# A fourth item buffer for VectorE in a windowed-attention and mixture-of-experts kernel

## The chip, the cores and the metric

The kernel runs on one core of one Trainium2 chip. Its metric is the device time in microseconds of one execution, from the first to the last instruction with what lies around them.

## The reference

The input is x of 8 x 1024 tokens with 128 channels. After a layer norm, the result is x plus an attention plus a mixture of experts. The attention is unusual: there are no queries and keys, but for each of 16 heads and each token a window of 64 earlier tokens, and for each pair a small network.

```
disp_win = windows(xn @ W_disp)            # 64 offsets per token, 16 values per head
strain   = disp_win - disp                 # token by token, offset by offset
bond     = gelu(strain @ W_strain + rel_emb @ W_pos) @ W_bond
damage   = sigmoid(gelu(strain @ W_dmg + b_dmg) @ W_dmg_out + b_dmg_out)
weights  = softmax(bond - 10 * damage)     # over the 64 offsets, masked at the start
attn     = (weights * val_win).sum(offsets) @ W_cproj
ffn      = sum over the 8 best of 160 experts of gate * silu(xn @ Wg) @ Wd, + a shared expert
out      = x + attn + ffn
```

## The kernel before

There is one program per engine, ordered by hand and tied by counting semaphores. It has a **token phase** (layer norm, projections, routing, to some 310 us), a short slot computation, the **first half** of the attention (half 0, 349 to some 1600 us), the **expert phase**, and the **second half** (half 1, from 2160 us). The token phase also writes zeros over xslot_dram, which the scatters of half 0 later fill.

An attention half handles 8 chunks of 512 tokens, each in two **steps**, one for each group of 8 heads. Steps are counted through, 0 to 15 in half 0 and 16 to 31 in half 1. The first and last steps of a half are written out; the middle ten are a loop of two steps (an even and an odd one) run five times, so that in each half four even steps, 6, 8, 10, 12 and 22, 24, 26, 28, begin behind a taken branch.

A step has 16 **items**, n = 0 to 15. An item is 8 offsets of one of the two networks (even n: bond, odd n: damage), a tile of 128 x 4096 fp32, 16 KB in each partition. It goes through three engines:

- the **subtraction** writes the item into a buffer: n%4 = 3 on GpSimd (u_pool, L954), the other three of four on VectorE (u_dve): as eight instructions of 512 columns, which also add the positional term (L1098, "STT" below), or as one of 4096 (L1093, "TT"); in half 1 items 6 and 14 use the latter and get the term in ScalarE (BIASED);
- ScalarE applies the gelu in place (L1021, L1023, or L1017 for those two);
- TensorE multiplies by the small output vectors (L1190, 8 matmuls, shown as x16) and raises item_done. It takes items in order, so item_done counts items 0, 1, 2, ... of all steps.

A VectorE buffer is free again when TensorE has done the item in it. The rule before is one buffer for each place in the group of four, and a wait for the item four places back:

```
return u_dve[:, (n % 4 - sum(q < n % 4 for q in on_pool))]      # item_buffer
return n - 3                                                    # buffer_free
```

Between items the engines do the rest of the attention, at fixed places of the same order. The places that matter here:

- **here** (L1168), on TensorE behind item 12: it puts the tokens' own values of the next step into ps_here, from which VectorE subtracts. It waits for all of this step's VectorE subtractions, and item 0 of the next step waits for it (here_done).
- **lg** (L1111), on VectorE behind items 0, 4, 8, 12: joins bond and damage logits of a group of four items; waits for ScalarE's tanh (L1005).
- **turn 0** (L1230, L1236), on TensorE behind item 4: brings logits of the step before into token order, into the one PSUM tile ps_u; turns 1 to 3 (L1238) stand behind items 5, 6, 7, and each waits until VectorE has emptied ps_u (tokens_in).
- **mx** and **ml** (L1120, L1125), on VectorE at places 7, 8, 9, 10: maximum and subtraction of the softmax, each behind its turn. The subtractions of items 8, 9 and 10 stand between them. Ahead of the first, at place 6, stand two small instructions (oinv L1129, o_sb L1133), and in half 1 the sum of eight gathered expert rows (add_routed, L1064, L1068, L1074), which stands behind item 14 too.
- **band transposes** (L1253), on TensorE from place 8: they use ps_u too, and the first waits for the fourth ml. ScalarE copies them out (L1037) behind its gelu of item 9 and on.

The zero-fill of xslot_dram (L315) is issued by SyncE once in each of the 16 chunks of the token phase and counted by slots_zeroed, for which GpSimd waits at the start of half 0.

Of the kernel before, what the change touches and what calls it, by code (L numbers as in the profile page):

```python
# [19 lines left out]
F32 = mybir.dt.float32  # L20
# [7 lines left out]
P = 128  # L28
# [11 lines left out]
def moe_attention_layer(nc, x, w_dispT, w_val, relT, w_strain, w_pos, w_bond, w_dmg, b_dmg,  # L40
# [28 lines left out]
    with ExitStack() as ctx:  # L69
# [42 lines left out]
        def sb(name, shape, dt=F32, c=ctx):  # L112
            return c.enter_context(nc.sbuf_tensor(name, shape, dt))
# [1 line left out]
        ident = sb("ident", [P, P])  # L115
        gates_all = sb("gates_all", [P, NBLK * TOPK])
        slots_all = sb("slots_all", [P, NBLK * TOPK])
        w1 = sb("w1", [P, 2 * HG, P])
        wval_sb = sb("wval_sb", [P, C])
        wr_sb = sb("wr_sb", [P, NE])  # L120
        bias_sb = sb("bias_sb", [P, NE])
        wgs_sb = sb("wgs_sb", [P, I])
        wds_sb = sb("wds_sb", [I, C])
        wc_sb = sb("wc_sb", [P, C])
# [8 lines left out]
        tile_id = sb("tile_id", [P, 6])  # L133
        mhalf = sb("mhalf", [P, J])

        zero = sb("zero", [P, 2048])
        slots_zeroed = sem("slots_zeroed")
        routing = ctx.enter_context(ExitStack())
        ranks_all = sb("ranks_all", [P, NCH * J, NE], F32, routing)
# [109 lines left out]
        with ExitStack() as c:  # L249
# [48 lines left out]
            with nc.Block() as block:  # L298
                @block.sync
                def _(sp):  # L300
                    def load(it, u):
                        sp.dma_start(xin[:, u], chunk_rows(x_rows, it)).then_inc(x_loaded[u], 16)

                    def body(k, last=False):
                        for u in range(2):
                            it = k * 2 + u
                            if not (last and u == 1):

                                if some(k + u):
                                    sp.wait_ge(x_free[1 - u], k + u)  # L310
                                load(it + 1, 1 - u)
                            sp.wait_ge(xn_ready, J * it + J)
                            sp.dma_start(chunk_rows(xn_dram, it), xn[:]).then_inc(stored["xn"], 16)

                            sp.dma_start(xslot_dram[bass.ds(it * ZR * P, ZR * P), :]  # L315
                                         .rearrange("(p n r) c -> p n (r c)", p=P, n=3),
                                         zero[:, 0:ZR * C // 3].unsqueeze(1).to_broadcast([P, 3, ZR * C // 3]))\
                                .then_inc(slots_zeroed, 16)
                            sp.wait_ge(part_ready, it + 1)
                            sp.dma_start(chunk_rows(part_dram, it), part_sb[:]).then_inc(stored["part"], 16)  # L320

                    load(0, 0)
                    ahead(sp, NCH // 2, body)
                    for s in stored.values():
                        sp.wait_ge(s, 16 * NCH)

                @block.gpsimd
                def _(pool):
# [307 lines left out]
        routing.close()  # L636


        NI = 16
        CH = 4  # L640
        NSTEP = 2 * NCH
# [24 lines left out]
        gate_done, hidden_done, down_done = sem("gate_done"), sem("hidden_done"), sem("down_done")  # L666
        ys_ready = sem("ys_ready")

        u_dve = sb("u_dve", [P, 3, 8, TC])
        u_pool = sb("u_pool", [P, 2, 8, TC])  # L670
        s_win = sb("s_win", [P, HG, 2, SW])
        tanh_sb = sb("tanh_sb", [P, 2, TC])
# [27 lines left out]
        def attention(half):  # L700
# [40 lines left out]
            def item_buffer(n):  # L741

                if n % 4 in on_pool:
                    return u_pool[:, (pool_of[n] - 1) % 2]
                return u_dve[:, (n % 4 - sum(q < n % 4 for q in on_pool))]

            def buffer_free(n):

                if n % 4 in on_pool:
                    return n + 1 - 8 // NP  # L750
                return n - 3

            def sync(sp):
                def load_windows(b, tc, it, par):
# [154 lines left out]
            def gpsimd(pool):  # L909
                if half == 0:  # L910
                    pool.memset(v_one[:], 1.0).then_inc(v_zeroed, 1)
                    pool.wait_ge(v_zeroed, 1)
                    pool.wait_ge(slots_zeroed, 16 * NCH)

                def spread(it):

                    pool.wait_ge(v_loaded, 16 * 2 * J * (it + 1))

                    if some(16 * it):
                        pool.wait_ge(av_done, 16 * it)  # L920
                        pool.sem_inc(held, 1)
                    pool.tensor_copy(v_one[:, :, :, 0:HS], v_raw[:].rearrange("p w (h e) -> p w h e", h=H))\
                        .then_inc(v_spread, 1)

                def route(s, par, j):

                    pool.wait_ge(slots_here, s + 1)
                    pool.sem_inc(held, 1)
                    if half == 0:
                        pool.wait_ge(rows_in, 16 * (s + 1))  # L930
                        pool.sem_inc(held, 1)
                        for i in range(j * TOPK, (j + 1) * TOPK):
                            pool.indirect_dma_start(  # L933
                                xslot_dram, bass.IndirectOffsetOnAxis(ap=slot_now[:, par, i:i + 1], axis=0),
                                xr[:, par, j, :], None).then_inc(scattered[par], 16)
                    else:

                        if some(s - first):
                            pool.wait_ge(sum_round, 2 * ROUND * (s - first - 1) + ROUND * (j // 2 + 1))
                            pool.sem_inc(held, 1)  # L940
                        for i in range(j * TOPK, (j + 1) * TOPK):
                            pool.indirect_dma_start(  # L942
                                yg[:, i, :], None, yslot_dram,
                                bass.IndirectOffsetOnAxis(ap=slot_now[:, par, i:i + 1], axis=0)).then_inc(gathered[j], 16)

                def step(s, it, par, st):
                    for n in range(NI):
                        cgrp, d0, ty = offsets(n)
                        if "i" in st and n % 4 in on_pool:
                            if pool_of[n] == 1:  # L950
                                pool.wait_ge(win_loaded[par], 32 * it + 32)
                            if some(NI * s + buffer_free(n)):
                                pool.wait_ge(item_done, NI * s + buffer_free(n))
                            pool.tensor_tensor(  # L954
                                item_buffer(n), windows(par, ty, d0, 8),
                                s_win[:, par, ty, PAD:PAD + TC].unsqueeze(1).to_broadcast([P, 8, TC]),
                                ALU.subtract).then_inc(sub_pool, 1)
                        if "y" in st and n == 12:

                            if some(it - 1):  # L960
                                pool.wait_ge(y_copied, it - 1)
                            if some(16 * (it - 1)):
                                pool.wait_ge(part_loaded, 16 * (it - 1))
                            pool.tensor_tensor(y_sb[:], y_sb[:], part_t[:], ALU.add).then_inc(y_ready, 1)
                        if "i" in st and n % 4 == 3:
                            route(s, par, n // 4)
                        if "a" in st and n == 7 and par == 0:
                            spread(it - 1)

                steps(pool, step)  # L970
# [522 lines left out]
```

## Time and profile before

| | us |
|---|---|
| median of 3 runs | 3539.15 |
| lowest, highest | 3538.04, 3539.51 |
| the profiled execution, its own time | 3547.54 |
| its span, first to last instruction | 3545.7 |
| VectorE busy | 2789.8 (79%) |
| ScalarE busy | 2505.1 (71%) |
| TensorE busy | 2462.7 (69%) |
| GpSimd busy | 2329.5 (66%) |

Times in the trace are counted from the start of the span. A matmul's end is modelled. The profiler names what ended an engine's idle time behind an arrow; "issue" stands where it knows nothing that the engine waited for.

### The profile page before, as it was taken

To read this page: it belongs to the slowest core of one execution; us is meant where nothing else is said; L and a number is where in the kernel's file an instruction comes from. 1 tells how busy PE (TensorE), PEld (TensorE's weight loads), DVE (VectorE), ACT (ScalarE), POOL (GpSimd) and SP (SyncE) were. 2 spreads that over 40 slices of the span, in tenths; PEclk is the share of its full clock that TensorE was granted. 3 is DMA by queue.
4 is the path that set the end of the run, shared out by engine and by line. 5 is a ranking of instruction groups with operands and counts; after the bars stand their busy time and mean duration, and the time that the engine had idled before them with its cause. 6 is when DMAs were issued, how large, how long until landed. Compare 5 with 4: busy or idle time off the path is not lost.

```text
span 3545.7 us, 64286 instructions
## 1 busy us (share of the span) xinstructions
PE 2462.7 (69%) x21226; PEld 1194.3 (34%) x21226; DVE 2789.8 (79%) x4286; ACT 2505.1 (71%) x1717; POOL 2329.5 (66%) x1603
## 2 busy tenths in 40 slices
PE   4663567766677767677888886676777676767666
PEld 2441112222222222225667663222222222222224
DVE  6888998888898888873333447999989999999981
ACT  1110898988888888883333335989898988888982
POOL 1221888887888787863434346888787777777760
PEclk9896888888888889879999998888887888888985
DMA  6774122222222222227888883223232222223222
GB/s 246 286 291 149 41 72 83 81 91 82 99 84 81 77 85 85 87 75 223 243 245 243 243 245 107 84 82 94 81 108 77 87 75 85 80 85 90 81 83 75
DMA packets 366243, 435.33 MB, mean 123 GB/s; under 512 B 48673, under 2 KB 282993, under 8 KB 366066
## 3 DMA queue, kind: packets, MB, share of 16 engines
q1 hardware_dynamic: 284658, 278.53, 25.2%
q0 software_dynamic: 57216, 143.22, 12.3%
q10 hardware_dynamic: 24192, 11.02, 1.1%
q8 instruction: 136, 2.23, 0.3%
q14 instruction: 41, 0.34, 0.0%
HBM read 233.83 MB, written 198.77 MB: 122 GB/s over the span
## 4 chain that ended last, share of the span: by engine, by line
ACT 22%; DVE 20%; PE 16%; issue 15%; SPq 10%; DMA 2%; ACTq 0%; DVEq 0%; POOL 0%; POOLq 0%
PE ps L1190 11%; DVE u_dve L1098 8%; DVE u_dve L1093 7%; ACT u_dve L1023 7%; SPq L1297 5%; ACT u_pool L1021 5%; ACT u_dve L1021 4%; SPq L1298 3%; PE ps L1253 3%; SPq L1309 2%; ACT at_sb L1037 2%; DVE mx L1120 2%; DVE ps L1068 1%; ACT L1029 1%; DVE ml L1125 1%
## 5 line engine op out<-in xcount | busy, mean ns | idle before, releaser
L1098 DVE SCALAR_TENSOR_TENSOR u_dve<-s_win,rpos,ps_here 128x512 f32<-128x512 f32 x1792 | 1198.1, 742 | 161.3 <-PE ps L1190 112.4
L1190 PE MATMUL ps<-u_dve,wsel 128*32 128x512 f32 x6144 | 953.5, 749 | 404.4 <-ACT u_dve L1021 207.8
L954 POOL TENSOR_TENSOR u_pool<-s_win 128x4096 f32<-128x4096 f32 x128 | 1021.9, 7984 | 167.7 <-PE ps L1190 162.2
L1023 ACT ACTIVATE u_dve<-u_dve 128x4096 f32<-128x4096 f32 x224 | 810.1, 3616 | 57.4 <-DVE u_dve L1098 57.1
L1093 DVE TENSOR_TENSOR u_dve<-s_win,ps_here 128x4096 f32<-128x4096 f32 x160 | 703.8, 4416 | 62.9 <-PE ps L1190 62.9
L933 POOL DMA_INDIRECT xslot_dram<-xr,slot_now x512 | 497.4, 972 | 146.9 <-issue 145.4
L942 POOL DMA_INDIRECT yg<-yslot_dram,slot_now x512 | 485.7, 949 | 157.9 <-issue 147.0
L1021 ACT ACTIVATE u_dve<-u_dve,bdmg_sb 128x4096 f32<-128x4096 f32 x128 | 474.9, 3710 | 12.2 <-DVE u_dve L1093 11.7
L1021 ACT ACTIVATE u_pool<-u_pool,bdmg_sb 128x4096 f32<-128x4096 f32 x128 | 474.1, 3704 | 0.0
L1190 PEld LDWEIGHTS ps<-u_dve,wsel 128*32 128x32 f32 x6144 | 190.6, 125 | 816.0 <-issue 524.0
L1388 DVE TENSOR_TENSOR u_pool<-u_pool,ps 128x512 f32<-128x512 f32 x168 | 115.6, 688 | 338.3 <-ACT u_pool L1373 338.3
L1190 PE MATMUL ps<-u_pool,wsel 128*32 128x512 f32 x2048 | 279.2, 668 | 100.0 <-ACT u_pool L1021 100.0
L1037 ACT ACTIVATE at_sb<-ps 128x512 f32<-128x512 f32 x256 | 150.9, 590 | 240.6 <-PE ps L1253 177.0
L1366 ACT ACTIVATE u_pool<-ps_here 128x512 f32<-128x512 f32 x168 | 100.3, 597 | 280.7 <-PE ps_here L1320 280.7
L1253 PE MATMUL ps<-ident,band 128*128 128x128 f32 x1024 | 210.0, 337 | 123.4 <-issue 102.2
L1253 PEld LDWEIGHTS ps<-ident,band 128*128 128x128 f32 x1024 | 148.8, 199 | 387.6 <-issue 349.5
L1403 POOL DMA_DIRECT2D yslot_dram<-u_dve x168 | 128.5, 765 | 215.0 <-DVE u_dve L1394 185.3
L1238 PE MATMUL ps<-ident,lg 128*128 128x128 f32 x384 | 75.9, 330 | 182.0 <-DVE ml L1125 182.0
L1298 POOL DMA_DIRECT2D u_dve<-in_w_expert x168 | 90.4, 538 | 151.5 <-issue 105.8
L1158 PEld LDWEIGHTS ps<-v_one,at_sb 128*64 128x64 f32 x4096 | 156.3, 151 | 97.6 <-issue 77.3
L1346 PE MATMUL ps<-u_dve,u_pool 64*128 64x64 f32 x2688 | 187.1, 279 | 0.4 <-DVE u_pool L1388 0.4
L1333 PE MATMUL ps<-u_pool,u_dve 128*64 128x128 f32 x2688 | 186.5, 282 | 0.0
(144 smaller groups left out, 2929.2 us busy)
## 6 DMA issues: line engine op xcount, KB each, us to landing
band<-band_dram SPq DMA_DIRECT2D x32, 2048.0 KB
xslot_dram<-zero SPq DMA_DIRECT2D x16, 2688.0 KB, 9.1
u_dve<-xslot_dram SPq DMA_DIRECT2D x168, 256.0 KB, 3.5
yslot_dram<-u_dve POOLq DMA_DIRECT2D x168, 256.0 KB, 3.3
band_dram<-ml SPq DMA_DIRECT2D x64, 512.0 KB
u_dve<-in_w_expert SPq DMA_DIRECT2D x336, 64.0 KB, 2.8
s_win<-s_dram SPq DMA_DIRECT2D x64, 288.0 KB
s_dram<-s_sb POOLq DMA_DIRECT2D x16, 1024.0 KB, 4.7
```

What stands on the lines that cost most here:

```text
L933: pool.indirect_dma_start(xslot_dram, bass.IndirectOffsetOnAxis(ap=slot_now[:, par, i:i + 1], axis=0), xr[:, par, j, :], None).then_inc(sc ...
L942: pool.indirect_dma_start(yg[:, i, :], None, yslot_dram, bass.IndirectOffsetOnAxis(ap=slot_now[:, par, i:i + 1], axis=0)).then_inc(gathere ...
L954: pool.tensor_tensor(item_buffer(n), windows(par, ty, d0, 8), s_win[:, par, ty, PAD:PAD + TC].unsqueeze(1).to_broadcast([P, 8, TC]), ALU.s ...
L1021: act.activation(u, u, ACT.Gelu, bias=bdmg_sb[:]).then_inc(gelu_done, 1)
L1023: act.activation(u, u, ACT.Gelu).then_inc(gelu_done, 1)
L1037: act.activation(at_sb[:, k % 2].rearrange("p i t -> p (i t)"), ps_u[:], ACT.Copy)\
L1093: last = dve.tensor_tensor(item_buffer(n), windows(par, ty, d0, 8), here.unsqueeze(1).to_broadcast([P, 8, TC]), ALU.subtract)
L1098: last = dve.scalar_tensor_tensor(out=item_buffer(n)[:, d, :], in0=s_win[:, par, ty, d0 + d + 1:d0 + d + 1 + TC], scalar=rpos[:, d0 + d:d0 ...
L1190: last = pe.matmul(logit[32 * g:32 * g + 32, :], wsel[:, ty, q, :], item_buffer(n)[:, d, :], start=(q == 0), stop=(q == 3))
L1253: last = pe.transpose(ps_u[:, i * P:(i + 1) * P], band[:, k // 2, 4 * (k % 2) + i:BANDW:HH], ident[:])
L1298: e.dma_start(we[:, u, i, :], w_expert[bass.ds(row, 1)].rearrange("e p f -> p (e f)"))\
L1346: last = pe.matmul(ps_z[:, u % 2, half, i * I:(i + 1) * I], hs[rows, u % 2, i * P:(i + 1) * P], we[rows, u, i, I:2 * I], start=True, stop= ...
```

## The change

VectorE gets a fourth buffer. Its twelve items of a step take the four buffers in turn (items 0, 1, 2, 4 use buffers 0 to 3, items 5, 6, 8, 9 again, then 10, 12, 13, 14), and each waits for the item that was in its buffer, the fourth before it among VectorE's own. In terms of n: items 0, 4, 8, 12 waited for the item four places back and now wait for the one six back; the others waited four back and now wait for the one five back.

The room comes from four weight tiles and the zero tile of the token phase, which are allocated in a scope of their own that is closed before the attention's tiles are placed. For that the zero-fill must be over by then, so SyncE waits for slots_zeroed at the end of the token phase, and GpSimd no longer does at the start of half 0.

```
@@ allocations
-        w1 = sb("w1", [P, 2 * HG, P])
-        wval_sb = sb("wval_sb", [P, C])
-        wr_sb = sb("wr_sb", [P, NE])
-        bias_sb = sb("bias_sb", [P, NE])
...
-        zero = sb("zero", [P, 2048])
+        start = ctx.enter_context(ExitStack())
+        w1 = sb("w1", [P, 2 * HG, P], F32, start)
+        wval_sb = sb("wval_sb", [P, C], F32, start)
+        wr_sb = sb("wr_sb", [P, NE], F32, start)
+        bias_sb = sb("bias_sb", [P, NE], F32, start)
+        zero = sb("zero", [P, 2048], F32, start)
@@ end of the token phase, SyncE
                     for s in stored.values():
                         sp.wait_ge(s, 16 * NCH)
+                    sp.wait_ge(slots_zeroed, 16 * NCH)
@@ before the attention
         routing.close()
+        start.close()
...
-        u_dve = sb("u_dve", [P, 3, 8, TC])
+        u_dve = sb("u_dve", [P, 4, 8, TC])
@@ item_buffer
-                return u_dve[:, (n % 4 - sum(q < n % 4 for q in on_pool))]
+                return u_dve[:, (dve_of[n] - 1) % 4]
@@ buffer_free
-                return n - 3
+                return max(m for m in range(-NI, n) if m % 4 not in on_pool
+                           and (m // NI * ND + dve_of[m % NI]) == dve_of[n] - 4) + 1
@@ start of half 0, GpSimd
                     pool.wait_ge(v_zeroed, 1)
-                    pool.wait_ge(slots_zeroed, 16 * NCH)
```

No engine's instructions change their order. What moves is the waits. VectorE at the start of step 0, items 0 to 5, before (item 4 is the first row that waits for item_done):

```order
L1098 SCALAR_TENSOR_TENSOR u_dve<-s_win,rpos,ps_here 128x512 [waits here_done,win_loaded0]
L1098 SCALAR_TENSOR_TENSOR u_dve<-s_win,rpos,ps_here 128x512 x7
L1093 TENSOR_TENSOR u_dve<-s_win,ps_here 128x4096
L1098 SCALAR_TENSOR_TENSOR u_dve<-s_win,rpos,ps_here 128x512 x8
L1098 SCALAR_TENSOR_TENSOR u_dve<-s_win,rpos,ps_here 128x512 [waits item_done]
L1098 SCALAR_TENSOR_TENSOR u_dve<-s_win,rpos,ps_here 128x512 x7
L1093 TENSOR_TENSOR u_dve<-s_win,ps_here 128x4096 [waits item_done]
```

and now (the lines are three further down in the file):

```order
L1101 SCALAR_TENSOR_TENSOR u_dve<-s_win,rpos,ps_here 128x512 [waits here_done,win_loaded0]
L1101 SCALAR_TENSOR_TENSOR u_dve<-s_win,rpos,ps_here 128x512 x7
L1096 TENSOR_TENSOR u_dve<-s_win,ps_here 128x4096
L1101 SCALAR_TENSOR_TENSOR u_dve<-s_win,rpos,ps_here 128x512 x16
L1096 TENSOR_TENSOR u_dve<-s_win,ps_here 128x4096 [waits item_done]
```

Items 2 and 4 now stand in one row of sixteen without a wait, and item 5 is the first that waits. In all later steps every item still waits for item_done, for an earlier count, and item 0 still waits for here_done.

## Rows read from the trace of the kernel before

**Rows 1.** Page, part 1: busy time of each engine, share of the span.
```profile
PE 2462.7 (69%) x21226; PEld 1194.3 (34%) x21226; DVE 2789.8 (79%) x4286; ACT 2505.1 (71%) x1717; POOL 2329.5 (66%) x1603
```

**Rows 2.** Waits of VectorE over the span: us in total, times, longest us.
```profile
DVE u_dve L1098 <- PE ps L1190: 112.4, 43, 8.1
DVE u_dve L1093 <- PE ps L1190: 62.9, 40, 3.1
```

**Rows 3.** Timeline, VectorE, step 10: start us, us, instruction, [idle before, releaser].
```profile
1107.60 5.36 DVE L1098 SCALAR_TENSOR_TENSOR u_dve<-s_win,rpos,ps_here 128x512 f32<-128x512 f32 x8 [2.25 <-PE ps_here L1168]
1112.87 0.68 DVE L1111 SCALAR_TENSOR_TENSOR lg<-tanh_sb,ps 128x512 f32<-128x512 f32 x1
...
1133.22 5.36 DVE L1098 SCALAR_TENSOR_TENSOR u_dve<-s_win,rpos,ps_here 128x512 f32<-128x512 f32 x8 [6.29 <-PE ps L1190]
...
1139.09 4.42 DVE L1093 TENSOR_TENSOR u_dve<-s_win,ps_here 128x4096 f32<-128x4096 f32 x1
1143.42 5.35 DVE L1098 SCALAR_TENSOR_TENSOR u_dve<-s_win,rpos,ps_here 128x512 f32<-128x512 f32 x8
...
1149.42 0.68 DVE L1120 TENSOR_REDUCE mx<-ps 128x8 f32<-128x512 f32 x1
```

**Rows 4.** Timeline, TensorE, step 10: items 14, 0, 1, turn 0, first band transpose.
```profile
1117.98 3.51 PE L1190 MATMUL ps<-u_dve,wsel 128*32 128x512 f32 x16
...
1129.51 3.64 PE L1190 MATMUL ps<-u_dve,wsel 128*32 128x512 f32 x16 [3.75 <-issue]
...
1135.18 3.44 PE L1190 MATMUL ps<-u_dve,wsel 128*32 128x512 f32 x16 [1.06 <-ACT u_dve L1023]
...
1145.37 1.05 PE L1236 MATMUL ps<-ident,lg 128*128 128x128 f32 x8
...
1170.43 0.88 PE L1253 MATMUL ps<-ident,band 128*128 128x128 f32 x3 [4.13 <-issue]
```

**Rows 5.** Timeline, ScalarE, step 10: gelu of item 4.
```profile
1138.61 3.62 ACT L1023 ACTIVATE u_dve<-u_dve 128x4096 f32<-128x4096 f32 x1
```

**Rows 6.** Timeline, VectorE, step 24: item 0, start of add_routed, first mx.
```profile
2800.50 5.35 DVE L1098 SCALAR_TENSOR_TENSOR u_dve<-s_win,rpos,ps_here 128x512 f32<-128x512 f32 x8 [0.28 <-issue]
...
2838.99 0.60 DVE L1064 TENSOR_SCALAR ps<-yg,gate_now 128x128 f32<-128x128 f32 x2
...
2843.58 0.68 DVE L1120 TENSOR_REDUCE mx<-ps 128x8 f32<-128x512 f32 x1
```

**Rows 7.** Timeline, TensorE, step 24: items 14, 0, 1, turn 0.
```profile
2809.89 1.92 PE L1190 MATMUL ps<-u_dve,wsel 128*32 128x512 f32 x16 [0.83 <-ACT u_dve L1017]
...
2820.52 3.16 PE L1190 MATMUL ps<-u_dve,wsel 128*32 128x512 f32 x16 [3.41 <-issue]
...
2824.56 1.93 PE L1190 MATMUL ps<-u_dve,wsel 128*32 128x512 f32 x16
...
2836.04 1.05 PE L1236 MATMUL ps<-ident,lg 128*128 128x128 f32 x8
```

**Rows 8.** Timeline, turn 0 and first mx of steps 17 and 31.
```profile
2269.70 1.05 PE L1236 MATMUL ps<-ident,lg 128*128 128x128 f32 x8
2273.03 0.68 DVE L1120 TENSOR_REDUCE mx<-ps 128x8 f32<-128x512 f32 x1
...
3409.79 1.05 PE L1236 MATMUL ps<-ident,lg 128*128 128x128 f32 x8
3412.01 0.68 DVE L1120 TENSOR_REDUCE mx<-ps 128x8 f32<-128x512 f32 x1
```

**Rows 9.** Busy time by stretch, steps 22 and 24: length, PE, PEld, DVE, ACT, POOL, granted clock.
```profile
2630.00:2716.00 86.00, 59.96 (x447) 22.07 (x444) 75.97 (x106) 72.32 (x48) 63.92 (x38) 0.78 0.28 81
2797.00:2879.00 82.00, 54.63 (x446) 20.53 (x442) 73.82 (x98) 70.78 (x48) 62.84 (x38) 0.88 0.29 85
```

**Rows 10.** Timeline, SyncE's queue: last zero-fill and the last store of the token phase.
```profile
291.19 0.57 SPq L315 DMA_DIRECT2D xslot_dram<-zero  x1
306.71 0.38 SPq L320 DMA_DIRECT2D part_dram<-part_sb  x1
```

## The prediction, written before the changed kernel ran

> **What bounds the kernel now.** I read the page's busy times first, then VectorE's waits, then the timeline of single steps. VectorE is busiest, but with 79% of the span it has holes [rows 1]. Of these the change can touch only the waits for an item's buffer: 112.4 us ahead of the STT subtractions and 62.9 us ahead of the TT ones, 175.3 us together [rows 2]. That is a ceiling and not a gain, since VectorE waits again for other things; the question is where its lateness holds someone up.
>
> So follow one step. Step 10 begins with item 0 at 1107.60, when ps_here is there. VectorE then waits 6.29 us for the buffer of item 4 [rows 3]. That wait ends with item 0 on TensorE, at 1129.51 + 3.64 = 1133.15 [rows 4]. TensorE was late with it because of 3.75 us put down to "issue" [rows 4]; steps 6, 8, 10, 12 and 22, 24, 26, 28, all behind the loop's branch, have it, and the same place in the straight-line even steps has not. VectorE is then busy without a hole until its first mx at 1149.42 [rows 3]. But turn 0, for which that mx waits, was done at 1145.37 + 1.05 = 1146.42 [rows 4]. VectorE is **3.00 us late** at the one place where it is the bound. From here four mx and ml pairs with items 8, 9, 10 between them run on VectorE without a hole, while TensorE waits for each; the first band transpose starts at 1170.43 after 4.13 us of idleness [rows 4], 21.0 us behind the first mx. Behind it ScalarE leads again, up to the next turn 0: it does the gelu of item 4 at 1138.61, at the end of item 3's, and the turn follows item 4 [rows 5]. So a step's period is ScalarE's chain up to turn 0, plus what VectorE is late, plus the fixed 21 us and the way to the next "here". In every step the distances other than the lateness differ by at most 2 to 4 us.
>
> I took turn 0's end and the start of the first mx in all 31 steps that have them. A step without lateness has 0.04 us between them. **Lateness:** steps 6, 8, 10, 12: 3.27, 2.87, 3.00, 3.01. Steps 17, 18, 19, 20, 21, 30, 31: 2.28, 3.10, 1.32, 3.09, 1.31, 2.69, 1.17 (the first is 2273.03 less 2270.75, the last 3412.01 less 3410.84) [rows 8]. Step 22: 6.92; 24, 26, 28: 6.49, 6.52, 6.56 (2843.58 less 2837.09 in step 24 [rows 6, 7]). Steps 23, 25, 27, 29: 0.29 or 0.30. All others 0.04, but for steps 1 and 2 with 0.6, where VectorE works without a buffer wait.
>
> **The change part by part.** *The fourth buffer, step 10.* An STT item takes 5.27 us from start to start, lg 0.68, a TT item 4.33 (1139.09 to 1143.42) [rows 3]. Item 0 at 1107.60, with its lg to 1113.6. Item 1 asks for item 12, done before "here": to 1117.9. Item 2 asks for item 13, which stands ahead of item 14 (from 1117.98 [rows 4]): to 1123.2. Item 4 asks for item 14, done at 1121.49 [rows 4], no wait: with lg to 1129.1, against 1139.1 before. Item 5 asks for item 0, done at 1133.15: to 1137.5. Item 6 asks for item 1, done at 1135.18 + 3.44 = 1138.62 [rows 4]: to 1143.9. The two small instructions (0.73, from 1143.42 + 5.27 to 1149.42) end at 1144.7. Turn 0 is done at 1146.42, so the first mx starts there: **all 3.0 us of lateness go**, and 1.7 us of waiting at turn 0 take their place. Steps 6, 8, 12 come out alike: 12.15 less 4 x 0.04 = 12.0 us.
>
> *Step 24.* Item 0 at 2800.50 [rows 6], lg to 2806.4, item 1 to 2810.8, item 2 to 2816.0, item 4 (item 14 done at 2811.81 [rows 7]) with lg to 2822.0, item 5 from the end of item 0 at 2823.68 to 2828.0, item 6 (TT here; item 1 done at 2826.49) to 2832.3, the small ones to 2833.1, add_routed 4.59 (2838.99 to 2843.58 [rows 6]) to 2837.7. Turn 0 is done at 2837.09, so 0.6 of 6.49 stays and 5.9 go. Steps 24, 26, 28: 17.6. Step 22 by the same steps: 5.6.
>
> *The seven steps with 1.17 to 3.10.* The same working clears turn 0 by 1 us or more in each: 14.96 less 7 x 0.04 = 14.7. The four with 0.29: 1.0. **Sum: 12.0 + 17.6 + 5.6 + 14.7 + 1.0 = 50.9 us.**
>
> *Why no more.* Item 0 of a step still waits for "here", behind item 12, so VectorE's lead ends with each step. Steps with no lateness gain nothing: their buffer waits become waits at turn 0. Behind the first mx the places are fixed.
>
> *What hides the rest.* The earlier writes lie beside ScalarE and GpSimd, as they do now. Per step GpSimd is busy 62.8 to 63.9 us of 82 to 86 [rows 9]; a step of 77 still holds that and its issue gaps. SyncE's new wait costs nothing: the last zero-fill is issued at 291.19, and a store that SyncE waits for anyway only at 306.71 [rows 10]; if a fill took longer than those 15 us, the rest would show once. GpSimd's dropped wait was long fulfilled. No instruction is added or moved, and the expert phase still uses buffers 0 to 2.
>
> *A rule beside the 3.75 us.* In the steps behind the branch item 0 is late by 3.75 and 3.41 us of "issue" [rows 4, 7], and I leave that in. The Trainium skill ("Runtime: NRT & Kernel Launch", Instruction fetch mechanics) says that a taken branch to a target outside the window held makes the engine fetch the page before it goes on. By that rule the stall is TensorE's own and stays, which gives the sum above; were it a hidden wait for VectorE, the sum would be that of the second rival.
>
> **From the sum to the time.** The sum is made in an execution of 3547.54 us by its own time (span 3545.7), 8.4 over the median; the steps have no reason to differ, so I subtract from the median: 3539.15 - 50.9 = **3488 us**.
>
> **The rivals.** *Forecast*, 42 to 62 us saved. The one unknown is TensorE's clock. Step 22 ran at a granted clock of 0.78, step 24 at 0.88 (1 being 2.4 GHz, one half 1.2) [rows 9]; counted from "here", with which these stretches begin, turn 0 ends at 41.9 us in one and 40.0 in the other, and VectorE would be ready for it at 43.2 or 40.7. If 24, 26, 28 fell to 22's level, 3 x 2.5 us of the gain would go; if eight or nine steps rose to 24's, 1.9 us each, 16 us would come on top. Chance 0.67.
>
> *More:* the stall behind the branch goes too. At most 8 x 3.6 = 29 us more, 3459. Against it: it stands only behind the branch. With the lucky clocks (3472) chance 0.08.
>
> *Part:* ScalarE or TensorE slips as VectorE comes early (an item at 3.64 us instead of 1.92 ahead of turn 0 costs 1.7 [rows 4, 7]), and half the gain stays, 3514. For it: items 0 and 1 in step 10 did run at 1.2 GHz behind an idle stretch. Chance 0.17.
>
> *Nothing:* VectorE's new lead is held elsewhere, at "here" or in a numbering of the buffers that gives no slack. But the order shows a wait less at items 2 and 4, and 12 items fit four buffers three times, so the counts match across steps. 3532 to 3546, chance 0.05.
>
> *Slower:* TensorE is given 1.2 GHz in item 4 and turn 0 of most steps. Item 4 would take 1.7 us more, the turn's two parts (twice about 1.0 [rows 4]) up to 2.0 more: 3.7 us a step, 115 us in 31 steps, 3603. From the 14th such step on it outweighs the gain. What speaks against it: between turn 0 and the band transposes TensorE will idle less and not more. The Trainium skill ("TensorE: Matmul & The Clock Gate", Part 1) ties the clock to how busy the array has been lately, so by it the clock would sooner rise, which no row here can settle. Chance 0.03.
>
> **The numbers.** A measurement tells 0.2%, 7 us, from no change. Faster: 0.67 + 0.08 + 0.17 = 0.92; same 0.05; slower 0.03. The range goes from the lucky clocks, 3472, to just over half the gain, 3512, and leaves out some 0.15.
>
> **What would show it.** In the changed profile VectorE's waits for L1190 should fall from 175 to under 100 us, and its waits ahead of mx for turn 0, 16 us now, should rise to some 80. The first mx should start 0.04 us behind turn 0 in all steps but 1, 2, 22, 24, 26, 28. From first mx to the band transposes 21 us must stay. I am wrong if turn 0 itself moves away from "here", if the mx is still late, or if the stall behind the branch changes.

## The result, and the profile after

| | before | changed |
|---|---|---|
| median | 3539.33 us (3538.04 to 3543.06, 4 runs) | 3499.12 us (3496.29 to 3502.86, 4 runs) |
| ratio | | 0.9883 (0.987 to 0.9895) |
| profiled execution | 3547.54 us | 3499.09 us |
| its span | 3545.7 us | 3497.3 us |
| granted clock, mean of the profiled execution | 0.866 | 0.871 |

The change saves 40.2 us, 1.2%; the interval of the ratio makes that 37 to 46 us. I had forecast 3488 us, and 3499 lies inside the range, though the saving is just under the 42 to 62 us that the prediction called its forecast. So the sign and the order of size came out, and 11 us of the 51 did not. The rest of this document asks which step of the sum those 11 us belong to.

Busy time, from part 1 of the page of the changed kernel (share of the span and instructions), against [rows 1]:

```profile
PE 2444.4 (70%) x21226; PEld 1194.6 (34%) x21226; DVE 2786.9 (80%) x4286; ACT 2500.7 (72%) x1717; POOL 2326.3 (67%) x1603
```

The counts are the same and VectorE's work is the same (2786.9 against 2789.8 us). What went is idle time. VectorE's waits in the changed kernel (total us, times, longest us; L1123, L1096, L1101, L1193 and L1239 are L1120, L1093, L1098, L1190 and L1236 of before):

```profile
DVE mx L1123 <- PE ps L1239: 101.2, 25, 7.9
...
DVE u_dve L1096 <- PE ps L1193: 26.2, 13, 4.6
...
DVE u_dve L1101 <- PE ps L1193: 12.3, 10, 1.9
```

The wait at turn 0 in the kernel before:

```profile
DVE mx L1120 <- PE ps L1236: 16.0, 10, 3.3
```

Against [rows 2], the waits for an item's buffer fell from 175.3 to 38.5 us, while 101.2 us are now waited at turn 0, where it had been 16.0. So of 137 us of buffer waits that vanished, 85 stand again at turn 0. This is why a sum of waits is no forecast.

Step 10 of the changed kernel on VectorE (start us, us, instruction, idle before with its releaser), to be laid beside [rows 3]:

```profile
1108.76 5.36 DVE L1101 SCALAR_TENSOR_TENSOR u_dve<-s_win,rpos,ps_here 128x512 f32<-128x512 f32 x8 [2.41 <-PE ps_here L1171]
1114.03 0.68 DVE L1114 SCALAR_TENSOR_TENSOR lg<-tanh_sb,ps 128x512 f32<-128x512 f32 x1
1114.63 4.42 DVE L1096 TENSOR_TENSOR u_dve<-s_win,ps_here 128x4096 f32<-128x4096 f32 x1
1118.96 10.62 DVE L1101 SCALAR_TENSOR_TENSOR u_dve<-s_win,rpos,ps_here 128x512 f32<-128x512 f32 x16
1129.87 0.69 DVE L1114 SCALAR_TENSOR_TENSOR lg<-tanh_sb,ps 128x512 f32<-128x512 f32 x1 [0.29 <-ACT tanh_sb L1008]
1134.94 4.42 DVE L1096 TENSOR_TENSOR u_dve<-s_win,ps_here 128x4096 f32<-128x4096 f32 x1 [4.38 <-PE ps L1193]
1140.53 5.36 DVE L1101 SCALAR_TENSOR_TENSOR u_dve<-s_win,rpos,ps_here 128x512 f32<-128x512 f32 x8 [1.18 <-PE ps L1193]
...
1148.36 0.69 DVE L1123 TENSOR_REDUCE mx<-ps 128x8 f32<-128x512 f32 x1 [1.75 <-PE ps L1239]
```

Items 2 and 4 now run as one block of 16 instructions: item 4 waits for nothing. Item 5 waits 4.38 us for item 0, and item 6 waits 1.18 us for item 1. The first mx waits 1.75 us for turn 0; the working had said 1.7. The TensorE side of the same step, beside [rows 4]:

```profile
1131.23 3.64 PE L1193 MATMUL ps<-u_dve,wsel 128*32 128x512 f32 x16 [3.60 <-DVE lg L1114]
...
1136.83 3.64 PE L1193 MATMUL ps<-u_dve,wsel 128*32 128x512 f32 x16 [0.99 <-issue]
...
1147.27 1.05 PE L1239 MATMUL ps<-ident,lg 128*128 128x128 f32 x8
...
1169.39 1.09 PE L1256 MATMUL ps<-ident,band 128*128 128x128 f32 x4 [4.12 <-issue]
```

Item 0 still stands behind a stall of 3.60 us. It bears another label now, "DVE lg", but it is at the same place and has the same length as the 3.75 us of "issue" before; the third experiment tells whose it is. From the first mx (1148.36) to the start of the first band transpose (1169.39; the row holds its four matmuls) it is 21.0 us, as before. But turn 0 ends at 1148.32, 39.56 us after the start of item 0 at 1108.76. Before it was 1146.42 less 1107.60, or 38.82 us. **Turn 0 has moved away from "here" by 0.7 us in this step**, which the prediction named as a sign that its sum would be wrong.

Step 24 on VectorE and then on TensorE, beside [rows 6] and [rows 7]:

```profile
2802.87 8.75 DVE L1096 TENSOR_TENSOR u_dve<-s_win,ps_here 128x4096 f32<-128x4096 f32 x2 [2.69 <-PE ps L1193]
...
2816.85 0.68 DVE L1123 TENSOR_REDUCE mx<-ps 128x8 f32<-128x512 f32 x1
```

```profile
2799.27 3.55 PE L1193 MATMUL ps<-u_dve,wsel 128*32 128x512 f32 x16 [3.89 <-issue]
...
2814.31 1.05 PE L1239 MATMUL ps<-ident,lg 128*128 128x128 f32 x8
```

The lateness is 2816.85 less 2815.36, or 1.49 us, where 6.49 stood before and I had left 0.6. VectorE's part came as worked out: items 5 and 6 start with the end of item 0 at 2802.82. Turn 0 came 0.9 us closer to that end than before (12.5 us behind it, against 13.4).

Over all steps I took the same marks as for the prediction. "Lateness" is the start of the first mx less the end of turn 0. "Stretch" is the time from the first step's "here" to the last step's of a half (steps 0 to 15, and 16 to 31), so it leaves out the last step of each half. In us, worked out from the traces (where the record of a matmul is missing at the end of turn 0, its usual length is taken):

| trace | lateness, half 0 | lateness, half 1 | "here" to turn 0, half 0, sum | stretch, half 0 | stretch, half 1 |
|---|---|---|---|---|---|
| before | 13.7 | 42.7 | 604.0 | 1151.1 | 1207.1 |
| changed | 1.7 | 3.8 | 609.5 | 1147.6 | 1165.0 |

The lateness fell from 56.4 to 5.5, by 50.9 us: to the tenth what the sum had said. Of steps 1 to 31, every one but 1, 2, 22, 24, 26 and 28 now has its first mx some 0.04 us behind turn 0, as forecast. Half 1's stretch fell by 42.1. Half 0's lateness fell by 12.0 and its stretch by only 3.5. Turn 0 came 7.7 us later in the sum of steps 1 to 14, which the stretch holds; with step 15, which lies outside it and where turn 0 came 2.2 us sooner, that is the 5.5 of the table. Whether this is the change's doing or scatter of single traces, one pair can't say.

### The profile page after: what moved, and what is told of

Its sections match the earlier page's. It is cut to its first block, busy times and chain, and to the rows that moved or that the text cites. A ratio compares the mean times of both kernels' runs of the same rounds, so it can differ in the third digit from the quotient of the medians.

```text
span 3497.3 us, 64286 instructions
## 1 busy us (share of the span) xinstructions
PE 2444.4 (70%) x21226; PEld 1194.6 (34%) x21226; DVE 2786.9 (80%) x4286; ACT 2500.7 (72%) x1717; POOL 2326.3 (67%) x1603
## 4 chain that ended last, share of the span: by engine, by line
ACT 24%; PE 19%; DVE 16%; issue 15%; SPq 11%; DMA 1%; ACTq 0%; DVEq 0%; POOLq 0%; POOL 0%
PE ps L1193 12%; ACT u_dve L1026 7%; DVE u_dve L1101 7%; ACT u_pool L1024 6%; DVE u_dve L1096 5%; SPq L1300 5%; ACT u_dve L1024 4%; SPq L1301 3%; PE ps L1256 3%; ACT at_sb L1040 2%; SPq L1312 2%; DVE mx L1123 2%; ACT u_dve L1020 1%; PE ps L1161 1%; ACT L1032 1%
## 5 line engine op out<-in xcount | busy, mean ns | idle before, releaser
L1101 DVE SCALAR_TENSOR_TENSOR u_dve<-s_win,rpos,ps_here 128x512 f32<-128x512 f32 x1792 | 1195.5, 741 | 64.5 <-PE ps_here L1171 36.6
L1193 PE MATMUL ps<-u_dve,wsel 128*32 128x512 f32 x6144 | 926.0, 730 | 419.6 <-ACT u_dve L1024 207.9
L1096 DVE TENSOR_TENSOR u_dve<-s_win,ps_here 128x4096 f32<-128x4096 f32 x160 | 703.6, 4414 | 26.2 <-PE ps L1193 26.2
L1193 PEld LDWEIGHTS ps<-u_dve,wsel 128*32 128x32 f32 x6144 | 188.4, 124 | 823.3 <-issue 514.9
L1193 PE MATMUL ps<-u_pool,wsel 128*32 128x512 f32 x2048 | 281.2, 672 | 108.6 <-ACT u_pool L1024 108.5
L1161 PE MATMUL ps<-v_one,at_sb 128*64 128x9 f32 x4096 | 178.1, 214 | 0.6 <-ACT at_sb L1040 0.6
```

Of the source, the lines that this page charges most:

```text
L1096: last = dve.tensor_tensor(item_buffer(n), windows(par, ty, d0, 8), here.unsqueeze(1).to_broadcast([P, 8, TC]), ALU.subtract)
L1101: last = dve.scalar_tensor_tensor(out=item_buffer(n)[:, d, :], in0=s_win[:, par, ty, d0 + d + 1:d0 + d + 1 + TC], scalar=rpos[:, d0 + d:d0 ...
L1161: last = pe.matmul(ps_o[tokens, j, h, :], at_sb[:, k % 2, i, tokens], v_one[:, 2 * j + half, h0 + h, :], start=True, stop=True)
L1193: last = pe.matmul(logit[32 * g:32 * g + 32, :], wsel[:, ty, q, :], item_buffer(n)[:, d, :], start=(q == 0), stop=(q == 3))
```

## The experiments

All ratios are to the kernel before, run on the same chip beside them, with 95% intervals. The expectations name two or three theories each time; the word is theirs.

**The kernel before once more, and the changed kernel with the old permission.** The first has no edit. It asks how far one trace of before can be trusted, since the profiled execution was 8.4 us over the median. The second keeps the fourth buffer, the rooms given back and the moved wait for the zero-fill, and only asks for a buffer as late as before:

> The kernel before once more, for its scatter and a second profile of it. The changed kernel's execution with a profile took 3499.1 us, the one of before 3547.5, 48 us apart, while the medians differ by 40. Theory 1: the profile of before was a slow one by some 8 us, because TensorE's clock fell differently in single steps; this run then gives 3535 to 3544, and in its trace the lateness of the first mx behind turn 0 sums to less than the 56 us of the first trace, or turn 0 stands nearer to here. Theory 2: recording a profile costs the kernel before 8 us and the changed one nothing; this trace then shows the same 56 us of lateness and the same distances to within 2 us in sum.

```diff
 def buffer_free(n):
     if n % 4 in on_pool:
         return n + 1 - 8 // NP
-    return max(m for m in range(-NI, n) if m % 4 not in on_pool
-               and (m // NI * ND + dve_of[m % NI]) == dve_of[n] - 4) + 1
+    return n - 3
```

> Four buffers in turn and everything else of the change, but each item waits as before, for the item four places back. Theory 1 (the earlier permission to write is the whole gain): within 5 us of the kernel before, 3534 to 3544, with some 12 us of lateness in steps 6, 8, 10, 12 and some 40 in the second half. Theory 2 (part of the gain is from where the tiles lie, or from the moved wait for the zero-fill): 5 to 40 us faster than before.

The kernel before again took 3543.22 us (3539.26 to 3553.13, 10 runs), ratio 0.9998 (0.9985 to 1.0011), and the 19 runs of before beside it had a median of 3543.62. Its second trace has 56.7 us of lateness, 13.1 in half 0 and 43.6 in half 1, and stretches of 1155.0 and 1204.2. So the lateness repeats to 0.3 us in total, while a whole execution lies anywhere in 3537 to 3553. Neither theory is decided: the lateness is the same, as theory 2 wants, but the way from "here" to turn 0 is 3.6 us longer in half 0, and the profiled execution was again a long one (3548.56). The three runs with a median of 3539.15, from which I had subtracted, were at the lower end of the scatter. Two later groups of runs of the kernel before have medians of 3542.08 (15) and 3540.32 (7); all 45 together have 3541.65.

With the old permission it is 3543.58 us (10 runs), ratio 0.9994 (0.9982 to 1.0006), lateness 56.7 and stretches 1151.6 and 1204.3. VectorE's waits, in the trace with the old permission:

```profile
DVE u_dve L1100 <- PE ps L1192: 109.1, 40, 7.3
...
DVE u_dve L1095 <- PE ps L1192: 61.0, 36, 3.1
...
DVE mx L1122 <- PE ps L1238: 18.9, 10, 3.3
```

These are the waits of before. The new places in the memory, the rooms given back and the zero-fill's wait bring and cost nothing that can be measured (the interval leaves room for 6 us saved or 2 lost); **the gain is the earlier permission to write**.

**TensorE's loop written out, in both kernels.** The prediction left the stall in the steps behind the branch alone. Here TensorE's program has no loop over its steps, the other engines keep theirs:

```diff
-def steps(e, step):
+def steps(e, step, written_out=False):
...
-    with e.Fori(it0 + 2, it0 + NCH // 2 - 1) as it:
+    if written_out:
+        for it in range(it0 + 2, it0 + NCH // 2 - 1):
+            for par in range(2):
+                step(it * 2 + par, it, par, ("iesat", "iesaty")[par])
+    else:
+        with e.Fori(it0 + 2, it0 + NCH // 2 - 1) as it:
...
-                steps(pe, step)
+                steps(pe, step, written_out=True)
```

> Three buffers, with TensorE's loop over the middle steps written out, so that no branch stands ahead of item 0; the other engines keep their loops. Theory 1 (the 3.4 to 3.8 us of issue ahead of item 0 are a stall of the branch, and they make most of VectorE's lateness): the stall is gone in all eight steps, lateness is 0.04 in steps 6 to 12 and some 3 in steps 22 to 28, 26 us less in sum, 3513 us (3505 to 3522). Theory 2 (the stall is a hidden wait for another engine): it stays, and the time is that of before, 3539. Theory 3 (written-out code must be fetched as well, and stalls elsewhere): the stall moves to other places, 3530 to 3560.

> Four buffers, with TensorE's loop over the middle steps written out. Theory 1: the fourth buffer has already taken the stall off the path except for the 0.2 to 1.5 us of lateness left in steps 22, 24, 26, 28, so writing the loop out brings 3 to 8 us, 3491 to 3496, and against three buffers written out the fourth buffer is worth only 15 to 25 us instead of 40. Theory 2: the stall still holds turn 0 by way of ScalarE's waits, and without it some 20 us more go, under 3485.

The kernel before with it: 3521.63 us (3520.09 to 3525.34, 4 runs), ratio 0.9937 (0.9917 to 0.9958). The changed kernel with it: 3492.93 us (3489.45 to 3495.46), ratio 0.9852 (0.983 to 0.9873). TensorE in step 10 of the first of the two, item 0 and turn 0:

```profile
1124.57 1.92 PE L1195 MATMUL ps<-u_dve,wsel 128*32 128x512 f32 x16 [0.95 <-ACT u_dve L1028]
...
1142.66 1.05 PE L1241 MATMUL ps<-ident,lg 128*128 128x128 f32 x8
```

The stall is gone: item 0 waits 0.95 us for ScalarE and runs in 1.92 us instead of 3.64. In all eight steps that had the stall, item 0 now waits 0.94 to 1.29 us for ScalarE, in both kernels. So it was TensorE's own and came with its loop, whatever label it bore, and was no wait for VectorE's lg. The Trainium skill ("Runtime: NRT & Kernel Launch", Instruction fetch mechanics) says that a taken branch to a target outside the window held stalls the engine for a fetch. This run agrees in that the stall goes with the branch; that a fetch fills it, no run here shows. Lateness in half 0 falls to 1.7 us here without a fourth buffer, since item 4's buffer is freed by item 0. In half 1 30.4 of 42.7 us stay.

Hence the two causes overlap. Against the 3543.62 of before, the loop alone brings 22.0 us and the fourth buffer alone 44.5 (40.2 against the runs beside it); both bring 50.7, and not the sum. With the loop written out the fourth buffer is worth 3521.63 - 3492.93 = 28.7 us, more than the 15 to 25 of theory 1. These were run beside each other, and the lateness falls by 29.7 us between them, from 32.1 to 2.4: here nearly all of it arrives. Of the fourth buffer's gain in the kernel with the loop, 12 to 16 us only made good what the branch did.

**The early permission in one half alone.** Half 0's 12 us were in doubt, so each half gets the new permission while the other keeps the old one:

```diff
 def buffer_free(n):
     if n % 4 in on_pool:
         return n + 1 - 8 // NP
+    if half == 1:
+        return n - 3
```

> The change with the earlier permission in the first half alone; in the second each item waits for the one four places back, as before. In the trace of the change the lateness of the first half fell by 12.0 us, but the stretch from its first to its last step got only 3.5 us shorter, since turn 0 moved 5.5 us in sum and two steps of the start took more. Theory 1 (given back: without the lateness TensorE runs more items at half clock ahead of turn 0, as it also did with three buffers and the loop written out): 3 to 8 us faster than before, ratio 0.998 to 0.999. Theory 2 (the 12 us are there, and the one trace had bad luck with the clock): 12 us faster, ratio 0.9966.

The other kernel has `half == 0` in that line.

> The change with the earlier permission in the second half alone. Its lateness fell by 38.9 us and the stretch from its first to its last step by 42 us in the traces. Theory 1: 34 to 42 us faster than before, ratio 0.9882 to 0.9904, so that nearly all of the measured gain of the change comes from here. Theory 2 (both halves give what their lateness says, 12 and 39 us, and something else costs 10): 28 to 32 us faster, ratio 0.991 to 0.992.

| kernel | median us (runs) | ratio | lateness, half 0 / 1 | "here" to turn 0, half 0 | stretch, half 0 / 1 |
|---|---|---|---|---|---|
| before beside them | 3542.08 (15) | 1 | | | |
| half 0 alone | 3537.07 (11) | 0.9988 (0.9979 to 0.9997) | 1.8 / 42.1 | 609.6 | 1147.6 / 1203.8 |
| half 1 alone | 3499.28 (4) | 0.9882 (0.9866 to 0.9897) | 10.8 / 4.7 | 607.3 | 1151.4 / 1164.9 |

Removing 12 us of lateness in half 0 makes the kernel 5.0 us faster; the interval is 1.1 to 7.4 us (0.0003 and 0.0021 of 3542.08), so 12 are excluded. Half 1 alone already has the ratio of the whole change (0.9882 against 0.9883, in different groups of runs), so on top of it half 0 brings nothing that four runs each can tell. VectorE's waits in the trace with half 0 alone show the middle state, part of the buffer waits already moved to turn 0:

```profile
DVE u_dve L1103 <- PE ps L1195: 68.2, 31, 7.3
...
DVE mx L1125 <- PE ps L1241: 68.1, 14, 7.9
...
DVE u_dve L1098 <- PE ps L1195: 43.0, 30, 4.5
```

Taken together, four traces with half 0's lateness (before, again, old permission, half 1 alone) have stretches of 1151.1, 1155.0, 1151.6 and 1151.4 there. Two that differ from these by half 0's permission alone (changed, half 0 alone) have 1147.6 both, 4.7 us less than the mean of the four; the two with the loop written out, which changes more than that, have 1145.3 and 1147.7. So **of the 12 us in half 0 some 7 do not arrive**, by the stretches as by the medians.

The traces show where they stay. Over steps 1 to 14 the lateness is 11.0 us less in the two than in the mean of the four, but the way from "here" to turn 0 is 5.8 us longer (567.4 against 561.6), and the way from the fourth ml to the next "here" 0.5 longer. The granted clock between "here" and turn 0 in these steps is 0.829 and 0.823 in the two, and 0.841 to 0.850 in the four.

Half 1 alone brings 42.8 us (36.5 to 47.5), at the upper end of the 34 to 42 of theory 1. Its stretches, 1204.9 in the mean of four traces with its lateness and 1165.0 and 1164.9 without, say 39.9.

Why turn 0 slips is only partly seen. In step 9 of the changed kernel it lies 41.9 us behind "here", and 40.0 before (single steps scatter: 43.5 in the second trace of before). TensorE's eight items ahead of it took 3.3 and seven times 1.9 us before, and 3.2, 1.9, 3.0, 1.9, 2.4, 3.6, 1.9, 1.9 us after: more of them at the lower clock of 1.2 GHz. What makes the clock fall for those items was not separated from the change of order in time. It is not the whole story either: with the loop written out in the kernel before, the clock there is 0.877 and the way to turn 0 is 4 us longer in sum all the same.

**What the new wait at turn 0 can buy.** VectorE now stands idle ahead of the first mx in 25 steps, and in the 21 us behind it TensorE waits for VectorE at each turn, since items 8, 9 and 10 lie between the four mx and ml pairs. With a fourth buffer item 8 asks for item 2, which is long done. So I moved item 8's subtraction ahead of the first mx, in the four-buffer kernel and in the three-buffer one:

```diff
 def step(s, it, par, st):
     for n in range(NI):
...
-        if "i" in st and n % 4 not in on_pool:
-            ...
+        if "i" in st and n % 4 not in on_pool and not (n == 8 and "s" in st):
+            subtract(s, it, par, n)
+        if "i" in st and "s" in st and n == 7:
+            subtract(s, it, par, 8)
```

> Four buffers, and VectorE does the subtraction of item 8 ahead of the first mx instead of behind it. With the change VectorE waits 101.2 us for turn 0 in 25 steps, up to 7.9 us in one. Theory 1 (the chain from turn 0 to the band transposes is bound by VectorE, so work taken out of it and put into that wait shortens the step): the way from turn 0 to the fourth ml falls from 20.9 us to about 18 in the steps that waited over 3 us and by about 1.4 us in the others, 35 to 50 us in all, 3449 to 3464. Theory 2 (ScalarE and TensorE set the pace of turns 1 to 3 as soon as VectorE is faster): under 15 us, 3485 or more. Theory 3 (a later first mx holds turn 1 and so TensorE's items): slower than the change.

> Three buffers, and item 8 ahead of the first mx. Here VectorE waits for turn 0 only 16 us in 10 steps, and in most steps of the second half it is late. Theory 1: only the few steps with a wait gain something, at most 16 us, 3523 to 3540, so the move needs the fourth buffer to be worth anything. Theory 2 (the move alone does it, since it lets turn 1 run while VectorE is at lg): 20 us or more, under 3519.

| kernel | median us (runs) | ratio | lateness | first mx to fourth ml, sum | stretch, half 0 / 1 |
|---|---|---|---|---|---|
| changed | 3499.12 (4) | 0.9883 | 5.5 | 648.3 | 1147.6 / 1165.0 |
| item 8 first, four buffers | 3428.16 (6) | 0.9694 (0.968 to 0.9709) | 84.2 | 507.0 | 1100.2 / 1143.0 |
| item 8 first, three buffers | 3558.52 (4) | 1.0054 (1.0038 to 1.007) | 203.4 | 503.8 | 1154.7 / 1223.0 |

With four buffers it brings 71 us more. The way from the first mx to the fourth ml falls from 20.9 to some 16.4 us a step, 141 in sum; VectorE's lateness rises by 79, and turn 0 comes 14 earlier: 76 us net in a trace that was the fastest of the six runs (3416.56). The theory that priced it highest had said 35 to 50 us; its mechanism came, its size was too small. Step 10, VectorE, item 8 first and four buffers:

```profile
1113.30 5.34 DVE L1095 SCALAR_TENSOR_TENSOR u_dve<-s_win,rpos,ps_here 128x512 f32<-128x512 f32 x8
1118.57 0.68 DVE L1129 TENSOR_REDUCE mx<-ps 128x8 f32<-128x512 f32 x1
...
1120.79 0.69 DVE L1129 TENSOR_REDUCE mx<-ps 128x8 f32<-128x512 f32 x1 [0.15 <-PE ps L1247]
...
1133.76 0.69 DVE L1134 TENSOR_TENSOR ml<-ps,mx 128x512 f32<-128x512 f32 x1
```

The four pairs stand between 1118.57 and 1134.45, 15.9 us, since only items 9 and 10 lie between them. ScalarE, which works on what the band transposes bring, waits less for them. The changed kernel, and then this one:

```profile
ACT at_sb L1040 <- PE ps L1256: 176.3, 54, 16.2
```

```profile
ACT at_sb L1040 <- PE ps L1262: 131.6, 52, 16.5
```

With three buffers the same move is slower than the kernel before, by 0.5%. I had expected a gain there by either theory, so both fell. Item 8 then asks for item 4, whose matmuls stand right ahead of turn 0 on TensorE, so the subtraction can't start until turn 0 is nearly due. VectorE's waits in that trace:

```profile
DVE u_dve L1092 <- PE ps L1196: 120.6, 52, 7.2
...
DVE u_dve L1087 <- PE ps L1196: 68.3, 43, 3.1
...
DVE mx L1126 <- PE ps L1244: 19.5, 34, 1.2
```

That is 188.9 us of buffer waits and 203.4 us of lateness, where the same order with four buffers has 34.8 and 84.2. **The fourth buffer is worth 40 to 44 us in the old order and 3558.52 - 3428.16 = 130 us in this one.**

**The move with TensorE's loop written out, and more items moved.** The first of these has both edits shown above. The second moves items 8, 9 and 10 each one place forward, ahead of the first, second and third mx, so that nothing lies between the third pair and the fourth:

> Four buffers, item 8 ahead of the first mx, and TensorE's loop written out. With item 8 first, VectorE still waits 34.8 us for items' buffers, most of it in item 5 behind the branch (4.7 us at most), and it is late at turn 0 again (84 us in sum, of which about 5.3 in a step is item 8 itself). Theory 1 (VectorE is the bound in most steps, so a wait taken from it shortens the step): 10 to 25 us less than with the loop, 3403 to 3418. Theory 2 (ScalarE's chain is the bound again, and VectorE's waits cost nothing): within 5 us, 3423 to 3433.

```diff
-        if "i" in st and n % 4 not in on_pool and not (n == 8 and "s" in st):
+        if "i" in st and n % 4 not in on_pool and not (8 <= n <= 10 and "s" in st):
             subtract(s, it, par, n)
         if "i" in st and "s" in st and n == 7:
             subtract(s, it, par, 8)
+        if "i" in st and "s" in st and n in (8, 9):
+            ahead_of_mx = n + 1
+        else:
+            ahead_of_mx = None
...
+            if ahead_of_mx:
+                subtract(s, it, par, ahead_of_mx)
             dve.wait_ge(turned, 4 * (s - 1) + j + 1)
```

> As with item 8 ahead of the first mx, and the subtractions of items 9 and 10 ahead of the second and third mx too, so that only the small instructions stand behind turn 3. With item 8 first, the second mx waits 22.7 us for turn 1 in 36 places and nothing else in the chain waits. Theory 1 (the chain is bound by VectorE's own work, and a turn hides behind a subtraction wherever it stands): the waits move from the second mx to the fourth, and the time stays within 10 us of 3428. Theory 2 (holding ps_u longer delays turns 1 and 2 and with them TensorE's items 6 and 7 and ScalarE): 15 us or more slower, over 3443.

Item 8 first with the loop written out: 3416.87 us (3414.97 to 3418.95, 4 runs), ratio 0.9649 (0.9633 to 0.9666). That is 11.3 us less than with the loop, inside the 10 to 25 of theory 1, and the **fastest version found**. Three items forward: 3495.01 us (3491.83 to 3497.66), ratio 0.9867 (0.9851 to 0.9884), which is 67 us slower than item 8 alone, as theory 2 had it in kind. The trace shows where they go. The way from the first mx to the fourth ml is 520.7 us in sum, no shorter than 507.0, since items 9 and 10 lie within it in both orders. But they stand ahead of the second and third mx instead of the third and fourth, so the second and third ml come later, and with them the turns that follow. TensorE in step 10, the third turn, item 7, item 8:

```profile
1150.13 1.11 PE L1253 MATMUL ps<-ident,lg 128*128 128x128 f32 x4 [3.74 <-DVE ml L1140]
1151.18 3.64 PE L1205 MATMUL ps<-u_pool,wsel 128*32 128x512 f32 x16
...
1157.77 3.64 PE L1205 MATMUL ps<-u_dve,wsel 128*32 128x512 f32 x16
```

TensorE stands idle for 3.74 us ahead of this turn and then does items 7 and 8 in 3.64 us each. In step 10 of the version with item 8 alone moved it does not idle there, and both take 1.92; there it is item 6, behind an idle stretch of 2.39 us, that takes 3.56:

```profile
1124.18 0.66 PE L1247 MATMUL ps<-ident,lg 128*128 128x128 f32 x4
1124.77 1.92 PE L1199 MATMUL ps<-u_pool,wsel 128*32 128x512 f32 x16
...
1128.50 1.92 PE L1199 MATMUL ps<-u_dve,wsel 128*32 128x512 f32 x16
```

The mean granted clock is 0.860 with three items forward against 0.886. The way from "here" to turn 0 is 32 us longer in sum, and from the fourth ml to the next "here" 491.9 us against 456.5. No run separates the lower clock from the later turns.

## Why the prediction was right, and where it was off

*What bounds a step.* Right. The lateness of VectorE at turn 0, and not its waits, was what the change could take. It fell by 50.9 us, the sum forecast, in half 0 by 12.0 and in half 1 by 38.9. In total it repeats within 0.3 us in three traces of kernels that ask for buffers as late as before. That the sum agrees to the tenth is in part luck: step 22 kept 0.66 us where the working left 1.3, step 24 kept 1.49 where it left 0.6, and half 0's lateness alone lies between 10.8 and 13.7 in the four traces that have it.

*Why 0.6 us stay in step 24.* 1.49 stay there, and 0.66, 0.24 and 0.93 in steps 22, 26 and 28. VectorE came when the working said: its first mx starts 14.0 us behind the end of item 0, as in 2837.7 less 2823.68. Turn 0 came 0.9 us sooner than it had.

*The buffer waits.* They should fall under 100 and fell to 38.5. The waits at turn 0 should rise to some 80 and rose to 101.2. Too cautious both times, the same mechanism.

*The 21 us behind the first mx, the stall, the SyncE wait.* 648.2 us in sum before and 648.3 after; a stall of 3.60 and 3.89 us in steps 10 and 24, where it had been 3.75 and 3.41; nothing to be measured for the moved wait. As forecast.

*The rivals.* "More", in which the stall goes too, did not happen; the loop written out shows that only the branch's going removes it. "Part" happened in half 0 and not in half 1, and the measured 40.2 us lie between the lower end of the forecast (42) and this rival. The range held because it reached down to half the gain. "Nothing" is what the old permission shows, and the change is not that. "Slower" needed a lower clock in most steps; the mean went from 0.866 to 0.871.

*The step that was off*, first part: "in every step the distances other than the lateness differ by at most 2 to 4 us" was used as if they stayed as they were once the lateness went. The term of 12.0 us for half 0 measured 5.0 (1.1 to 7.4) by the medians and 4.7 by the stretches, because turn 0 came 5.8 us later in the sum of steps 1 to 14. The prediction had named a turn 0 that moves away from "here" as a sign against it, and in half 0 that sign came.

*The step that was off*, second part: "the steps have no reason to differ, so I subtract from the median". The sum came from an execution 8.4 us over its median, and the changed kernel's profiled execution lies on its median. The spans of these two differ by 3545.7 - 3497.3 = 48.4 us, near the 50.9; the medians differ by 40.2. In this pair half 0's stretch brings 3.5 us and half 1's 42.1, and 3.6 come behind the last "here", where the prediction had 1.2 for step 31; it left out step 32, which has a turn 0 too and whose lateness fell from 3.16 to 1.60. The start was also low: 3539.15 was a median of 3 runs, and 45 have 3541.65. How much each part weighs can't be told from runs that scatter over 15 us. With 7 us off for half 0, the forecast would be 3495 us from the median beside the changed kernel and 3500 from the highest later one, 3543.62; measured is 3499.12.

*What stays open.* Why items ahead of turn 0 fall to 1.2 GHz more often once VectorE is early; it was seen in half 0, but no run changed it alone. And what a short execution of the kernel before does otherwise than a long one: its two traces, at 3547.54 and 3548.56 us, are both of long ones. A fifth buffer was not tried.

## What to carry to other kernels

Price another buffer by how late its writer is at the place where it is the last to come, and not by its waits for a buffer: 175 us of waits held 51 us of lateness, of which 40 to 45 arrived. Then look at the wait that takes its place. Here the new slack at turn 0, filled with one subtraction moved up, was worth more (71 us) than the buffer by itself, and without the buffer the same move was slower than no change. Moving two more was a loss again, so try the smallest move first.

## What the hardware showed that I had not expected

A stall stands on TensorE ahead of item 0 behind each pass of its loop: 3.41 to 4.83 us in the first trace of before, 3.08 to 5.21 over all nine traces that have the loop. It goes when the loop is written out (3543.62 to 3521.63 us; with four buffers 3499.12 to 3492.93; with item 8 first 3428.16 to 3416.87). The trace puts it down to "issue" or, in other kernels at the same place, to "DVE lg", so the label alone does not tell it from a wait.

Most of TensorE's items take 1.92 or 3.64 us, with a granted clock of 1.00 (2.4 GHz) in one of the first kind (2809.9 us in the trace of before) and of 0.50 (1.2 GHz) in one of the second (1151.2 us with three items forward); the others lie between. Where TensorE idles moved together with which of them are slow: 3.74 us of idleness ahead of one turn, then 3.64 us for each of the next two items. A reordering of VectorE's work that seems only to spread it better can so be lost on another engine.
